# The last row block of an attention kernel, ended in two halves

## The chip, the cores and the metric

The kernel runs on one core of a Trainium2 chip. The metric is the device time of one launch in microseconds (us); lower is better. Five instruction streams take part and meet only at semaphores: TensorE (PE), VectorE (DVE), ScalarE (ACT), GpSimd (POOL), and SyncE (SP), which here issues only DMAs.

## The reference

Two layers of graph attention over N = 4096 nodes with D = 64 features, each followed by a residual sum and a layer norm without scale or shift:

```python
src, dst = h @ a1, h @ a2
e = leaky_relu(src[:, None] + dst[None, :], 0.01)
e = where(adj > 0, e, -9e15)               # layer 2: -1e9
h_prime = softmax(e, axis=1) @ h           # layer 2: @ (x @ weight_w), then + bias
x = layernorm(x + h_prime)                 # each row of 64 by itself
```

`adj` is 4096 x 4096 int32, about one entry in a thousand being 1. Layer 2 has the same form with `wh = x @ weight_w` in place of `h`. The output is x after layer 2, 4096 x 64 float32.

## The kernel before

The leaky relu makes exp(e) a product of a row factor and a column factor, with one pair of factors where src + dst is positive and another where it is not. So the masked softmax is two products of a 0/1 matrix with a small table: `pos` holds the mask where the sum is positive, `neg` where it is negative. Both are byte matrices that TensorE reads as fp8. The table `xy` (in layer 2 it lies in the buffer named `stage`) holds features and a column of ones, times the column factor, split into three bf16 parts: 3 x 65 = 195 columns.

**Tiling.** The rows come in `NS` = 8 blocks `s` of 512 rows; each has `RB` = 4 row blocks `r` of 128 rows, and each row block has a PSUM bank of its own, `acc[:, r]`. The 4096 columns come in `NG` = 4 granules `g` of 1024, each of 8 tiles of 128 columns. The function `granule(layer, s, g)` is TensorE's work on one granule: for each of the 4 row blocks 8 tiles x 2 masks = 16 matmuls of 195 columns, each with a weight load, into that row block's bank. In this text a **unit** is the 16 matmuls of one granule and one row block; a block `s` is 16 units, in the order g = 0 with r = 0 to 3, then g = 1, and so on. A bank is complete when all four granules have been added.

**Who makes what in layer 2.** For each block and granule:

- ACT (`signs`) writes 8 activations of sign into `neg[:, g]`, and raises `signs_ready`.
- DVE (`mask`) turns them into the two masks: an AND at L832 gives `neg`, an XOR at L835 gives `pos`; each has 128 x 1024 words.
- PE (`granule`) waits for both masks of that granule, before its first matmul.

After the last granule of a block the DVE does the epilogue: `read_acc` (L841, one reduction of a bank each, when that bank's last unit is done), `average` (L859 to L868), `residual_sum` (L873), `moments` (L878 to L881, ending in `var`); POOL computes var to the power -1/2 (L994, `inverse_std`); the DVE normalizes into `x1s` (L891, `normalize1`); SP stores `x1s` with one DMA of 128 KB (L293 in the loop, L295 for the last block). Instructions of `average` and later work on all 4 row blocks at once where they can (L859, L863), and one at a time where they can't (x4 at L866, L873, L878, L880, L891).

**Order.** Every engine runs its stream in the order written; nothing is scheduled. The blocks 1 to 7 of layer 2 are a loop on PE (L503); the DVE has a loop over s = 1 to 6 (L968), in which the masks of block s + 1 are woven with the epilogue of block s:

```python
with dve.Fori(1, NS - 1) as s:
    mask(1, s, NG - 1)
    for g in range(NG):
        if g:
            mask(1, s + 1, g - 1)
        if g == 1:
            read_acc(1, s)
        if g == 2:
            average(1, s); residual_sum(1, s); moments(1, s)
    normalize1(s)
```

So while PE works on block 7, the DVE does in this order: the rest of `read_acc` of block 6, the masks of granule 1 of block 7, the epilogue of block 6 up to `var`, the masks of granule 2, `normalize1` of block 6, the masks of granule 3. The masks of granule 0 come ahead of all that.

Of the kernel before, what the change touches and what calls it, by code (L numbers as in the profile page):

```python
# [23 lines left out]
ALU = mybir.AluOpType  # L24
# [10 lines left out]
P = 128  # L35
# [3 lines left out]
EPS = 1e-5  # L39
# [3 lines left out]
def gat_kernel(nc, x, adj, a0, w1, a1, bias1, ident, out):  # L43
# [28 lines left out]
    CODES = 0x38383838  # L72
    FREE_AT_FIRST = RING * RB
    LINKS = 8

    ctx = ExitStack()
    with ctx:
# [167 lines left out]
        @block.sync  # L245
        def _(sp):
            sp.sem_inc(stored, 16)
            load_tiles(sp, LOWER)
            sp.dma_start(acol[:, 0:1], a0[0:D, :]).then_inc(s_a, 16)
            load_rows(sp, slice(0, RB))  # L250
            load(sp, LOWER, 0, 0)
            load_rows(sp, slice(RB, IB // 2))
            load(sp, LOWER, 0, 1)
            sp.dma_start(acol[:, 1:2], a1[0:D, :]).then_inc(s_w, 16)
            sp.dma_start(acol[:, 2:3], a1[D:2 * D, :]).then_inc(s_w, 16)
            sp.dma_start(wext1[0:D, 0:D], w1).then_inc(s_w, 16)
# [24 lines left out]

            for g in range(KEEP, NG):
                sp.wait_ge(spilled[g - KEEP], 16 * NS)
                sp.wait_ge(pos_ready, (NS - 1) * NG + g + 1)
                reload(0, g)
            with sp.Fori(1, NS) as s:
                for g in range(KEEP, NG):
                    sp.wait_ge(pos_ready, (NS + s - 1) * NG + g + 1)
                    sp.sem_inc(sp_turn, 1)
                    reload(s, g)  # L290
                sp.wait_ge(x1_ready, NS + s + 1)
                sp.sem_inc(sp_turn, 1)
                sp.dma_start(rows_of(out, s - 1, RB, P), x1s[:, :, :]).then_inc(stored, 16)  # L293
            sp.wait_ge(x1_ready, 2 * NS + 1)
            sp.dma_start(rows_of(out, NS - 1, RB, P), x1s[:, :, :]).then_inc(stored, 16)  # L295
            sp.wait_ge(stored, 16 * (NS + 1))


        @block.tensor
        def _(pe):  # L300
# [114 lines left out]
                                            start=True, stop=True)  # L415
                last.then_inc(wh_ready, 1)

            def granule(layer, s, g):
                k = (layer * NS + s) * NG + g
                pe.wait_ge(neg_ready, k + 1)  # L420
                pe.wait_ge(pos_ready, k + 1)
                pe.sem_inc(pe_turn, 1)
                pe.wait_ge(tables_ready, layer * NG + g + 1)
                masks = [m[:, g, :].bitcast(FP8).rearrange("p (b i e) -> p b e i", b=GB, e=BYTES) for m in (pos, neg)]
                for r in range(RB):
                    if g == 0:
# [73 lines left out]
            scores1(NS - 2, NS)  # L500
            for g in range(1, NG):
                granule(1, 0, g)
            with pe.Fori(1, NS) as s:  # L503
                for g in range(NG):
                    granule(1, s, g)


        @block.scalar
# [153 lines left out]
        def _(dve):  # L662
# [171 lines left out]
                    dve.wait_ge(neg_ready, k + 1)  # L834
                    nc.vector.tensor_tensor(words(pos[:, g, :]), a, c, ALU.bitwise_xor).then_inc(pos_ready, 1)  # L835

            def read_acc(layer, s):
                for r in range(RB):

                    dve.wait_ge(products, FREE_AT_FIRST + ((layer * NS + s) * NG + NG - 1) * RB + r + 1)  # L840
                    nc.vector.tensor_reduce(  # L841
                        red[:, r, :, :].rearrange("p c f -> p (c f)").rearrange("p (c f) -> p c f", c=2),
                        acc[:, r, 0:2 * XW].rearrange("p (c k f) -> p c f k", c=2, k=PARTS), AX, ALU.add)\
                      .then_inc(acc_read, 1)

            def link(layer, s, n, ins):

                ins.then_inc(epi, 1)
                dve.wait_ge(epi, (layer * NS + s) * LINKS + n)

            V = nc.vector
            blocks = range(RB)

            def average(layer, s):

                factors = ab[:, :, :].rearrange("p c (k r h) -> p k h r c", r=RB, h=2)[:, bass.ds(s // 2, 1), bass.ds(s % 2, 1)]
                dve.wait_ge(acc_read, (layer * NS + s) * RB + 2 * RB)
                dve.wait_ge(exp_ready, [3, 6][layer])
                link(layer, s, 1, V.tensor_tensor(  # L859
                    red[:, :, :, :], red[:, :, :, :],  # L860
                    factors.rearrange("p k h r c -> p (k h r) c").unsqueeze(3).broadcast_to((P, RB, 2, E)), ALU.mult))
                dve.wait_ge(x1_ready, layer * NS + s + 1)
                link(layer, s, 2, V.tensor_tensor(num[:, :, :], red[:, :, 0, :], red[:, :, 1, :], ALU.add))  # L863
                link(layer, s, 3, V.tensor_scalar(empty, num[:, :, D], 0.0, None, ALU.is_equal))
                V.tensor_tensor(total, num[:, :, D], empty, ALU.add)
                link(layer, s, 4, [V.scalar_tensor_tensor(y[:, r, :], meanv[:, layer, :], empty[:, r:r + 1], y[:, r, :],  # L866
                                                          ALU.mult, ALU.add) for r in blocks][-1])
                V.reciprocal(rden, total).then_inc(epi, 1)  # L868

            def residual_sum(layer, s):  # L870

                dve.wait_ge(epi, (layer * NS + s) * LINKS + 5)
                link(layer, s, 6, [V.scalar_tensor_tensor(y[:, r, :], y[:, r, :], rden[:, r:r + 1],  # L873
                                                          xn[:, row_at(s, r), :].rearrange("p o d -> p (o d)"),
                                                          ALU.mult, ALU.add) for r in blocks][-1])

            def moments(layer, s):
                link(layer, s, 7, [V.bn_stats(bn[:, r, :], y[:, r, :]) for r in blocks][-1])  # L878
                dve.sem_inc(dve_turn, 1)
                link(layer, s, 8, [V.bn_aggr(mv[:, r, :], bn[:, r, :]) for r in blocks][-1])  # L880
                V.tensor_scalar(var, mv[:, :, 1], EPS, None, ALU.add).then_inc(var_ready, 1)  # L881
                if layer == 0:
                    V.tensor_scalar(minus_mean, mv[:, :, 0], -1.0, None, ALU.mult).then_inc(mean_turned, 1)

            def normalize1(s):

                dve.wait_ge(stored, 16 * (s + 1))
                dve.wait_ge(std_ready, 2 * NS + s + 1)
                dve.sem_inc(dve_turn, 1)
                for r in blocks:  # L890
                    last = V.tensor_scalar(x1s[:, r, :], y[:, r, :], mv[:, r, 0:1], rstd[:, r:r + 1],  # L891
                                           ALU.subtract, ALU.mult)
                last.then_inc(x1_ready, 1)
# [84 lines left out]
                        moments(1, s)  # L978
                normalize1(s)
            mask(1, NS - 1, NG - 1)  # L980
            read_acc(1, NS - 1)
            average(1, NS - 1)
            residual_sum(1, NS - 1)
            moments(1, NS - 1)
            normalize1(NS - 1)


        @block.gpsimd
        def _(pool):
            def inverse_std(layer, s):  # L990

                pool.wait_ge(var_ready, layer * NS + s + 1)
                pool.sem_inc(pool_turn, 1)
                nc.gpsimd.tensor_tensor(rstd, var, minus_half[:, :], ALU.pow).then_inc(std_ready, 1)  # L994
                if layer == 1:
                    return
                pool.wait_ge(std_ready, 2 * s + 1)
# [18 lines left out]
                inverse_std(0, s)  # L1016
                positive(s + 1, 3)
            inverse_std(0, NS - 1)
            with pool.Fori(0, NS) as s:
                inverse_std(1, s)  # L1020


# [20 lines left out]
```

## Time and profile before

| what | value |
|---|---|
| times of 3 runs | 504.74, 500.26, 503.65 us; median 503.65 |
| the profiled execution | 500.48 us; its span from first to last instruction 498.5 us |
| busy in the span | PE 443.1, PEld 414.0, DVE 409.3, ACT 394.9, POOL 86.8 us |
| matmuls of layer 2 (`acc<-stage`) | 2048, mean 248 ns each as recorded |
| mean granted TensorE clock | 0.932 of full |

All rows are of the one profiled execution. The time that a launch takes is its span and about 2 us around it. Recorded matmuls overlap one another: their length is not their cost, the distance from one start to the next is. In the DVE's rows a mark in brackets at the end is idle time before the row, and what ended it. "PEclk" is the TensorE clock that was granted: 1.00 is 2.4 GHz and 0.50 is 1.2 GHz.

### The profile page before, as it was taken

How to read it: one execution, taken by the hardware profiler on the slowest of the kernel's cores; microseconds unless marked ns; L12 is line 12 of the kernel's file. 1: busy time of each engine (PE TensorE's matmuls, PEld its weight loads, DVE VectorE, ACT ScalarE, POOL GpSimd, SP SyncE). 2: the span in 40 equal slices, each digit the busy share in tenths (PEclk: the TensorE clock that was granted, in tenths of full speed). 3: DMA queues.
4: the chain of work that ended last, by engine and by line, in shares of the span. 5: the costliest groups of instructions: out<-in, count | busy, mean ns of one | idle time of the engine just before them, and what ended most of it. 6: DMA issues, size and time to landing. Idle time of an engine off the chain costs nothing.

```text
span 498.5 us, 11757 instructions
## 1 busy us (share of the span) xinstructions
PE 443.1 (89%) x4420; PEld 414.0 (83%) x4420; DVE 409.3 (82%) x736; ACT 394.9 (79%) x589; POOL 86.8 (17%) x60
## 2 busy tenths in 40 slices
PE   0799868888989999998997959999999999999991
PEld 0379767877979889897997846999999999999991
DVE  3789989889799898998989897968587786968755
ACT  2686179878878879888794956999999999999920
POOL 0012221513315142241512120001010110101010
PEclk9987979997979979899899966999999999999997
DMA  7999999999999999999992200203030302022000
GB/s 193 246 240 279 278 263 286 321 297 303 324 309 322 305 299 318 319 331 302 331 310 93 81 0 2 60 27 96 1 95 0 95 0 95 17 77 84 10 11 11
DMA packets 80290, 87.64 MB, mean 176 GB/s; under 512 B 7298, under 2 KB 76162, under 8 KB 80258
## 3 DMA queue, kind: packets, MB, share of 16 engines
q1 hardware_dynamic: 45602, 52.98, 37.5%
q10 hardware_dynamic: 34656, 34.21, 25.2%
q8 instruction: 23, 0.38, 0.3%
q14 instruction: 9, 0.07, 0.0%
HBM read 77.74 MB, written 9.44 MB: 175 GB/s over the span
## 4 chain that ended last, share of the span: by engine, by line
PE 42%; DVE 24%; DMA 18%; issue 12%; POOL 1%; SPq 1%; ACT 1%; DVEq 0%; ACTq 0%; POOLq 0%
PE acc L431 38%; DMA stage<-in_adj 17%; DVE narrow L803 4%; DVE turned L815 4%; DVE pos L829 2%; DMA xn<-in_x 2%; DVE num L873 2%; DVE num L866 1%; DVE red L859 1%; PE flip L361 1%; DVE bn L878 1%; DVE num L863 1%; DVE kept L740 1%; PE acc L330 1%; DVE kept L737 1%
## 5 line engine op out<-in xcount | busy, mean ns | idle before, releaser
L569 ACT ACTIVATE neg<-srow,dcol 128x512 int8<-128x512 f32 (+1 forms) x320 | 221.4, 866 | 11.1 <-issue 7.6
L431 PE MATMUL acc<-xy_old,pos 128*128 128x195 bf16 x1024 | 196.0, 261 | 18.3 <-POOL pos L1007 12.2
L431 PE MATMUL acc<-xy_old,neg 128*128 128x195 bf16 x1024 | 195.7, 261 | 0.0
L431 PE MATMUL acc<-stage,pos 128*128 128x195 bf16 x1024 | 177.3, 248 | 0.0
L431 PE MATMUL acc<-stage,neg 128*128 128x195 bf16 x1024 | 177.3, 248 | 0.0
L569 ACT ACTIVATE neg<-xy_old,dcol 128x512 int8 x192 | 137.4, 863 | 0.0
L431 PEld LDWEIGHTS acc<-xy_old,pos 128*128 128x128 fp8e4 x1024 | 106.5, 104 | 26.8 <-issue 25.2
L431 PEld LDWEIGHTS acc<-xy_old,neg 128*128 128x128 fp8e4 x1024 | 106.0, 104 | 1.3
L431 PEld LDWEIGHTS acc<-stage,pos 128*128 128x128 fp8e4 x1024 | 100.6, 98 | 0.0
L431 PEld LDWEIGHTS acc<-stage,neg 128*128 128x128 fp8e4 x1024 | 100.4, 98 | 0.1
L803 DVE TENSOR_SCALAR narrow<-stage 128x4096 uint8<-128x4096 int32 x32 | 74.1, 2314 | 16.7 <-DMA stage<-in_adj 15.9
L994 POOL TENSOR_TENSOR small<-small,minus_half 128x4 f32<-128x4 f32 x16 | 35.1, 2192 | 209.0 <-DVE small L881 209.0
L841 DVE TENSOR_REDUCE red<-acc 128x130 f32<-128x390 f32 x64 | 33.7, 554 | 34.6 <-PE acc L431 34.5
L1007 POOL TENSOR_TENSOR pos<-kept,neg 128x512 uint32<-128x512 uint32 x16 | 22.2, 1390 | 142.7 <-DVE neg L832 142.7
L832 DVE TENSOR_TENSOR neg<-neg,kept 128x1024 uint32<-128x1024 uint32 x32 | 39.1, 1223 | 7.3 <-ACT neg L569 6.6
L832 DVE TENSOR_TENSOR neg<-neg,turned 128x1024 uint32<-128x1024 uint32 x32 | 39.1, 1223 | 2.4 <-ACT neg L569 1.7
L1007 POOL TENSOR_TENSOR pos<-turned,neg 128x512 uint32<-128x512 uint32 x16 | 22.3, 1393 | 54.6 <-DVE neg L832 53.8
L577 ACT ACTIVATE xn<-num,small 128x64 f32 (+1 forms) x32 | 11.5, 430 | 16.6 <-POOL small L1000 16.6
L319 PE MATMUL acc<-idf,xn 128*64 128x128 f32 x32 | 7.2, 421 | 15.2 <-DMA xn<-in_x 15.2
L319 PEld LDWEIGHTS acc<-idf,xn 128*64 128x64 f32 x32 | 5.3, 173 | 17.7 <-issue 11.9
L835 DVE TENSOR_TENSOR pos<-kept,neg 128x1024 uint32<-128x1024 uint32 x16 | 19.6, 1225 | 0.5
L835 DVE TENSOR_TENSOR pos<-turned,neg 128x1024 uint32<-128x1024 uint32 x16 | 19.6, 1224 | 0.5
(121 smaller groups left out, 343.0 us busy)
## 6 DMA issues: line engine op xcount, KB each, us to landing
stage<-in_adj ACTq DMA_DIRECT2D x64, 512.0 KB, 9.2
stage<-in_adj SPq DMA_DIRECT2D x64, 512.0 KB, 9.4
spill<-turned SPq DMA_DIRECT2D x16, 512.0 KB, 7.6
turned<-spill SPq DMA_DIRECT2D x16, 512.0 KB, 3.9
out<-x1s SPq DMA_DIRECT2D x8, 128.0 KB, 1.9
xn<-in_x SPq DMA_DIRECT2D x1, 768.0 KB, 16.5
kept<-in_x SPq DMA_DIRECT2D x4, 128.0 KB, 3.8
kept<-in_x ACTq DMA_DIRECT2D x4, 128.0 KB, 5.0
```

The lines of the kernel that those rows point to most:

```text
L319: last = nc.tensor.transpose(acc[0:D, t % RB, b * P:(b + 1) * P], xn[:, t // 2 * (2 * RB) + t % 2 + 2 * b, :], idf[:, :])
L431: last = nc.tensor.matmul(acc[:, r, c * XW:(c + 1) * XW], masks[c][:, t // BYTES, t % BYTES, r * P:(r + 1) * P], xy[layer][:, g * GT + t, ...
L569: last = nc.scalar.activation(o[:, t // BYTES, t % BYTES, :], row, ACT.Sign, bias=dcol[:, layer, col:col + 1])
L577: last = nc.scalar.activation(xn[:, row_at(s, r), :].rearrange("p o d -> p (o d)"), y[:, r, :], ACT.Identity, bias=shift_n[:, r:r + 1], sc ...
L803: nc.vector.tensor_scalar(narrow[:, 0:GN].rearrange("p (b g j) -> p g b j", b=GB, g=GR), stage[:, g % SLOTS, :].rearrange("p (g b j) -> p ...
L815: nc.vector.transpose(words(mask_at(s, g)), words(narrow[:, 0:GN])).then_inc(turned_ready, 1)
L829: nc.vector.scalar_tensor_tensor(words(pos[:, g, :])[:, half], c[:, half], CODES, a[:, half], ALU.bitwise_xor, ALU.bitwise_and).then_inc(p ...
L832: nc.vector.tensor_tensor(c, c, a, ALU.bitwise_and).then_inc(neg_ready, 1)
L835: nc.vector.tensor_tensor(words(pos[:, g, :]), a, c, ALU.bitwise_xor).then_inc(pos_ready, 1)
L841: nc.vector.tensor_reduce(red[:, r, :, :].rearrange("p c f -> p (c f)").rearrange("p (c f) -> p c f", c=2), acc[:, r, 0:2 * XW].rearrange( ...
L994: nc.gpsimd.tensor_tensor(rstd, var, minus_half[:, :], ALU.pow).then_inc(std_ready, 1)
L1007: nc.gpsimd.tensor_tensor(pos[:, g, :].bitcast(U32)[:, half], mask_at(s, g).bitcast(U32)[:, half], neg[:, g, :].bitcast(U32)[:, half], ALU ...
```

## The change

The last block of layer 2 (s = 7) is taken out of PE's loop and written out, its 16 units in another order: eight pieces of two units, each a granule for the row blocks 0 and 1 (h = 0) or 2 and 3 (h = 1). The epilogue of this block, POOL's power and the store run twice, each for two row blocks. Functions get a parameter `part` or `rows`; for all other blocks they issue what they did before. The semaphore counts are raised by one step for the second part.

```diff
+    HALVES = (slice(0, RB // 2), slice(RB // 2, RB))
+    LAST_ORDER = ((0, 0), (1, 0), (2, 0), (0, 1), (3, 0), (1, 1), (2, 1), (3, 1))
...
-            sp.wait_ge(x1_ready, 2 * NS + 1)
-            sp.dma_start(rows_of(out, NS - 1, RB, P), x1s[:, :, :]).then_inc(stored, 16)
-            sp.wait_ge(stored, 16 * (NS + 1))
+            for h, part in enumerate(HALVES):
+                sp.wait_ge(x1_ready, 2 * NS + 1 + h)
+                sp.dma_start(rows_of(out, NS - 1, RB, P)[:, part], x1s[:, part, :]).then_inc(stored, 16)
+            sp.wait_ge(stored, 16 * (NS + 2))
...
-            def granule(layer, s, g):
+            def granule(layer, s, g, rows=range(RB)):
...
-                for r in range(RB):
+                for r in rows:
...
-            with pe.Fori(1, NS) as s:
+            with pe.Fori(1, NS - 1) as s:
                 for g in range(NG):
                     granule(1, s, g)
+            for g, h in LAST_ORDER:
+                granule(1, NS - 1, g, range(RB)[HALVES[h]])
...
-            def read_acc(layer, s):
-                for r in range(RB):
-
-                    dve.wait_ge(products, FREE_AT_FIRST + ((layer * NS + s) * NG + NG - 1) * RB + r + 1)
+            def read_acc(layer, s, part=every):
+                for r in range(RB)[part]:
+
+                    dve.wait_ge(products, finished(layer, s, r))
...
             mask(1, NS - 1, NG - 1)
-            read_acc(1, NS - 1)
-            average(1, NS - 1)
-            residual_sum(1, NS - 1)
-            moments(1, NS - 1)
-            normalize1(NS - 1)
+            for part in HALVES:
+                read_acc(1, NS - 1, part)
+                average(1, NS - 1, part)
+                residual_sum(1, NS - 1, part)
+                moments(1, NS - 1, part)
+                normalize1(NS - 1, part)
...
-            with pool.Fori(0, NS) as s:
+            with pool.Fori(0, NS - 1) as s:
                 inverse_std(1, s)
+            for part in HALVES:
+                inverse_std(1, NS - 1, part)
```

(`finished` counts in `LAST_ORDER` which unit completes a bank.)

TensorE before, the body of the loop over blocks: the first matmul of each unit that waits, with its number in the stream (`stage` is the table of layer 2). Granules 1, 2 and 3 begin at 2470, 2534 and 2598, 64 matmuls apart.

```order
2403 L431 MATMUL acc<-stage,pos 128x195 [waits neg_ready,pos_ready,tables_ready,acc_read]
...
2420 L431 MATMUL acc<-stage,pos 128x195 [waits acc_read]
...
2470 L431 MATMUL acc<-stage,pos 128x195 [waits neg_ready,pos_ready,tables_ready]
...
2534 L431 MATMUL acc<-stage,pos 128x195 [waits neg_ready,pos_ready,tables_ready]
...
2598 L431 MATMUL acc<-stage,pos 128x195 [waits neg_ready,pos_ready,tables_ready]
```

TensorE now, the last block behind the loop, in the same form; each row that waits for the masks begins a piece of `LAST_ORDER`.

```order
2664 L434 MATMUL acc<-stage,pos 128x195 [waits neg_ready,pos_ready,tables_ready,acc_read]
...
2696 L434 MATMUL acc<-stage,pos 128x195 [waits neg_ready,pos_ready,tables_ready]
...
2728 L434 MATMUL acc<-stage,pos 128x195 [waits neg_ready,pos_ready,tables_ready]
...
2760 L434 MATMUL acc<-stage,pos 128x195 [waits neg_ready,pos_ready,tables_ready,acc_read]
...
2792 L434 MATMUL acc<-stage,pos 128x195 [waits neg_ready,pos_ready,tables_ready]
...
2824 L434 MATMUL acc<-stage,pos 128x195 [waits neg_ready,pos_ready,tables_ready]
```

The first need of granule 1's masks has moved from 64 matmuls after the block's start to 32, that of granule 2's from 128 to 64, and that of granule 3's (2792) from 192 to 128. What makes the masks has not moved.

The DVE before, at the end of its stream: the masks of granule 3 of the last block, then its epilogue for all four row blocks.

```order
L832 TENSOR_TENSOR neg<-neg,turned 128x1024
L835 TENSOR_TENSOR pos<-turned,neg 128x1024
L841 TENSOR_REDUCE red<-acc 128x130 x4
L859 TENSOR_TENSOR red<-red,ab 128x520
L863 TENSOR_TENSOR num<-red 128x260
L864 TENSOR_SCALAR small<-num 128x4
L865 TENSOR_TENSOR small<-num,small 128x4
L866 SCALAR_TENSOR_TENSOR num<-meanv,small,num 128x64 x4
```

The DVE now, the same place: the first part, from the masks to the sum, and the end of it with the start of the second part.

```order
L837 TENSOR_TENSOR neg<-neg,turned 128x1024
L840 TENSOR_TENSOR pos<-turned,neg 128x1024
L859 TENSOR_REDUCE red<-acc 128x130 x2
L878 TENSOR_TENSOR red<-red,ab 128x260
L880 TENSOR_TENSOR num<-red 128x130
...
L883 SCALAR_TENSOR_TENSOR num<-meanv,small,num 128x64 x2
...
L898 TENSOR_SCALAR small<-mv 128x2
L908 TENSOR_SCALAR x1s<-num,mv,small 128x64 x2
L859 TENSOR_REDUCE red<-acc 128x130 x2
```

The first part's rows stand wholly ahead of the second part's; behind the last matmul stands only the second, with half the elements or half the instructions at each step.

## Rows read from the trace of the kernel before

**Rows 1.** The chain that ended last, by time: start us, us, what.
```profile
454.95 33.47 PE acc L431 x387
```

**Rows 2.** Timeline of DVE while PE works on block 7: start us, us, what.
```profile
466.31 0.57 DVE L841 TENSOR_REDUCE red<-acc 128x130 f32<-128x390 f32 x1 [0.82 <-PE acc L431]
...
468.04 1.22 DVE L835 TENSOR_TENSOR pos<-kept,neg 128x1024 uint32<-128x1024 uint32 x1
469.18 0.69 DVE L859 TENSOR_TENSOR red<-red,ab 128x520 f32<-128x520 f32 x1
...
474.17 1.22 DVE L832 TENSOR_TENSOR neg<-neg,turned 128x1024 uint32<-128x1024 uint32 x1
475.43 1.23 DVE L835 TENSOR_TENSOR pos<-turned,neg 128x1024 uint32<-128x1024 uint32 x1
...
478.71 1.22 DVE L835 TENSOR_TENSOR pos<-turned,neg 128x1024 uint32<-128x1024 uint32 x1
```

**Rows 3.** Timeline of ACT from 460 us on: its last 24 signs.
```profile
459.22 17.31 ACT L569 ACTIVATE neg<-xy_old,dcol 128x512 int8 x24
```

**Rows 4.** Timeline of PE and of POOL around waits in layer 1.
```profile
66.37 0.32 PE L431 MATMUL acc<-xy_old,pos 128*128 128x195 bf16 x1 [6.29 <-POOL pos L1007]
66.49 0.37 PE L431 MATMUL acc<-xy_old,neg 128*128 128x195 bf16 x1
...
68.45 0.37 PE L431 MATMUL acc<-xy_old,neg 128*128 128x195 bf16 x1
...
82.12 1.27 POOL L1007 TENSOR_TENSOR pos<-kept,neg 128x512 uint32<-128x512 uint32 x1 [10.31 <-DVE neg L832]
83.50 0.24 PE L431 MATMUL acc<-xy_old,pos 128*128 128x195 bf16 x1 [1.80 <-POOL pos L1007]
```

**Rows 5.** Windows of PE: stretch, its us, PE busy (matmuls), PEclk, DMA share, GB/s.
```profile
60.08:65.30 5.22, 0.00 (x0) 1.00 0.91 295
...
66.37:72.00 5.63, 5.63 (x35) 0.50 1.11 268
...
112.67:114.88 2.21, 0.00 (x1) 0.59 1.12 304
114.88:119.90 5.02, 5.02 (x32) 0.50 1.07 338
...
236.00:239.35 3.35, 3.35 (x23) 0.50 1.12 360
263.32:265.23 1.91, 0.00 (x1) 1.00 0.00 0
```

**Rows 6.** Timeline of DVE, POOL and the DMA queue at the end.
```profile
484.30 0.56 DVE L841 TENSOR_REDUCE red<-acc 128x130 f32<-128x390 f32 x1 [4.37 <-PE acc L431]
...
488.45 0.56 DVE L841 TENSOR_REDUCE red<-acc 128x130 f32<-128x390 f32 x1 [0.82 <-PE acc L431]
489.05 0.70 DVE L859 TENSOR_TENSOR red<-red,ab 128x520 f32<-128x520 f32 x1
489.78 0.43 DVE L863 TENSOR_TENSOR num<-red 128x260 f32<-128x260 f32 x1
...
490.53 0.86 DVE L866 SCALAR_TENSOR_TENSOR num<-meanv,small,num 128x64 f32<-128x64 f32 x4
...
491.64 0.87 DVE L873 SCALAR_TENSOR_TENSOR num<-num,small,xn 128x64 f32<-128x64 f32 x4
492.55 0.61 DVE L878 BATCH_NORM_STATS2 bn<-num 128x6 f32<-128x64 f32 x4
493.31 0.38 DVE L880 BATCH_NORM_AGGREGATE mv<-bn 128x2 f32<-128x6 f32 x4 [0.15 <-DVE bn L878]
...
494.07 1.01 POOL L994 TENSOR_TENSOR small<-small,minus_half 128x4 f32<-128x4 f32 x1 [17.81 <-DVE small L881]
495.21 0.98 DVE L891 TENSOR_SCALAR x1s<-num,mv,small 128x64 f32<-128x64 f32 x4 [1.32 <-POOL small L994]
496.22 0.40 SPq L295 DMA_DIRECT2D out<-x1s  x1
```

More of the change, by code:

```diff
@@ L835, in mask, with finished @@
                     nc.vector.tensor_tensor(words(pos[:, g, :]), a, c, ALU.bitwise_xor).then_inc(pos_ready, 1)
-            def read_acc(layer, s):
-                for r in range(RB):
-                    dve.wait_ge(products, FREE_AT_FIRST + ((layer * NS + s) * NG + NG - 1) * RB + r + 1)
+            every = slice(0, RB)
+            def finished(layer, s, r):
+                if layer == 1 and isinstance(s, int) and s == NS - 1:
+                    done = 0
+                    for g, h in LAST_ORDER:
+                        for q in range(RB)[HALVES[h]]:
+                            done += 1
+                            if (g, q) == (NG - 1, r):
+                                return FREE_AT_FIRST + (layer * NS + s) * NG * RB + done
+                return FREE_AT_FIRST + ((layer * NS + s) * NG + NG - 1) * RB + r + 1
+            def read_acc(layer, s, part=every):
+                for r in range(RB)[part]:
+                    dve.wait_ge(products, finished(layer, s, r))
                     nc.vector.tensor_reduce(
@@ L844, in read_acc, with link, average @@
                       .then_inc(acc_read, 1)
-            def link(layer, s, n, ins):
+            def link(layer, s, n, ins, part=every):
                 ins.then_inc(epi, 1)
-                dve.wait_ge(epi, (layer * NS + s) * LINKS + n)
+                dve.wait_ge(epi, (layer * NS + s) * LINKS + n + (LINKS if part == HALVES[1] else 0))
             V = nc.vector
-            blocks = range(RB)
-            def average(layer, s):
+            def average(layer, s, part=every):
+                n = part.stop - part.start
@@ L856, in average @@
                 factors = ab[:, :, :].rearrange("p c (k r h) -> p k h r c", r=RB, h=2)[:, bass.ds(s // 2, 1), bass.ds(s % 2, 1)]
-                dve.wait_ge(acc_read, (layer * NS + s) * RB + 2 * RB)
+                factors = factors.rearrange("p k h r c -> p (k h r) c")[:, part].unsqueeze(3).broadcast_to((P, n, 2, E))
+                dve.wait_ge(acc_read, (layer * NS + s) * RB + RB + part.stop)
                 dve.wait_ge(exp_ready, [3, 6][layer])
-                link(layer, s, 1, V.tensor_tensor(
-                    red[:, :, :, :], red[:, :, :, :],
-                    factors.rearrange("p k h r c -> p (k h r) c").unsqueeze(3).broadcast_to((P, RB, 2, E)), ALU.mult))
+                link(layer, s, 1, V.tensor_tensor(red[:, part, :, :], red[:, part, :, :], factors, ALU.mult), part)
@@ L862, in average @@
                 dve.wait_ge(x1_ready, layer * NS + s + 1)
-                link(layer, s, 2, V.tensor_tensor(num[:, :, :], red[:, :, 0, :], red[:, :, 1, :], ALU.add))
-                link(layer, s, 3, V.tensor_scalar(empty, num[:, :, D], 0.0, None, ALU.is_equal))
-                V.tensor_tensor(total, num[:, :, D], empty, ALU.add)
+                link(layer, s, 2, V.tensor_tensor(num[:, part, :], red[:, part, 0, :], red[:, part, 1, :], ALU.add), part)
+                link(layer, s, 3, V.tensor_scalar(empty[:, part], num[:, part, D], 0.0, None, ALU.is_equal), part)
@@ L866, in average @@
+                V.tensor_tensor(total[:, part], num[:, part, D], empty[:, part], ALU.add)
                 link(layer, s, 4, [V.scalar_tensor_tensor(y[:, r, :], meanv[:, layer, :], empty[:, r:r + 1], y[:, r, :],
[L867 to L872, printed above, removed]
+                                                          ALU.mult, ALU.add) for r in range(RB)[part]][-1], part)
@@ L873, in residual_sum @@
+                V.reciprocal(rden[:, part], total[:, part]).then_inc(epi, 1)
+            def residual_sum(layer, s, part=every):
+                dve.wait_ge(epi, (layer * NS + s) * LINKS + 5 + (LINKS if part == HALVES[1] else 0))
                 link(layer, s, 6, [V.scalar_tensor_tensor(y[:, r, :], y[:, r, :], rden[:, r:r + 1],
                                                           xn[:, row_at(s, r), :].rearrange("p o d -> p (o d)"),
-                                                          ALU.mult, ALU.add) for r in blocks][-1])
@@ L877, in moments @@
-            def moments(layer, s):
-                link(layer, s, 7, [V.bn_stats(bn[:, r, :], y[:, r, :]) for r in blocks][-1])
+                                                          ALU.mult, ALU.add) for r in range(RB)[part]][-1], part)
+            def moments(layer, s, part=every):
+                link(layer, s, 7, [V.bn_stats(bn[:, r, :], y[:, r, :]) for r in range(RB)[part]][-1], part)
                 dve.sem_inc(dve_turn, 1)
-                link(layer, s, 8, [V.bn_aggr(mv[:, r, :], bn[:, r, :]) for r in blocks][-1])
-                V.tensor_scalar(var, mv[:, :, 1], EPS, None, ALU.add).then_inc(var_ready, 1)
+                link(layer, s, 8, [V.bn_aggr(mv[:, r, :], bn[:, r, :]) for r in range(RB)[part]][-1], part)
+                V.tensor_scalar(var[:, part], mv[:, part, 1], EPS, None, ALU.add).then_inc(var_ready, 1)
@@ L882, in moments, with normalize1 @@
                 if layer == 0:
                     V.tensor_scalar(minus_mean, mv[:, :, 0], -1.0, None, ALU.mult).then_inc(mean_turned, 1)
-            def normalize1(s):
+            def normalize1(s, part=every):
                 dve.wait_ge(stored, 16 * (s + 1))
-                dve.wait_ge(std_ready, 2 * NS + s + 1)
+                dve.wait_ge(std_ready, 2 * NS + s + 1 + (1 if part == HALVES[1] else 0))
                 dve.sem_inc(dve_turn, 1)
-                for r in blocks:
+                for r in range(RB)[part]:
@@ L980, in _, with inverse_std @@
             mask(1, NS - 1, NG - 1)
-            read_acc(1, NS - 1)
-            average(1, NS - 1)
-            residual_sum(1, NS - 1)
-            moments(1, NS - 1)
-            normalize1(NS - 1)
+            for part in HALVES:
[4 more added lines that the diff above has]
+                normalize1(NS - 1, part)
         @block.gpsimd
         def _(pool):
-            def inverse_std(layer, s):
-                pool.wait_ge(var_ready, layer * NS + s + 1)
+            def inverse_std(layer, s, part=slice(0, RB)):
+                pool.wait_ge(var_ready, layer * NS + s + 1 + (1 if part == HALVES[1] else 0))
                 pool.sem_inc(pool_turn, 1)
-                nc.gpsimd.tensor_tensor(rstd, var, minus_half[:, :], ALU.pow).then_inc(std_ready, 1)
+                nc.gpsimd.tensor_tensor(rstd[:, part], var[:, part], minus_half[:, part], ALU.pow).then_inc(std_ready, 1)
                 if layer == 1:
```

## The prediction

> **What bounds the kernel now.** I read the end of the chain that ended last first, since the change touches only the last block. From 454.95 us on, 33.47 us of the chain are matmuls of L431 without a break [rows 1]; behind them come the last reduction and the epilogue [rows 6]. So two stretches set the end: the sixteen units of block 7 on PE, and the tail behind the last of them.
>
> The pace of PE comes from the four reductions of block 7. Each starts as soon as its bank is complete, the first at 484.30 and the fourth at 488.45 us [rows 6]: 4.15 / 3 = 1.383 us a unit, 86.4 ns a matmul, sixteen units 22.1 us. The fourth reduction of block 6 starts at 466.31 us [rows 2], and 466.31 + 22.13 = 488.44: PE goes through block 7 without waiting. Then comes the tail: from 488.45 to the store's issue at 496.22 us are 7.77 us [rows 6], and 2.28 us more to the end of the span at 498.5.
>
> The second thing to read is when the masks of block 7 become ready. In its timeline the DVE ends the XOR of granule 1 at 468.04 + 1.22 = 469.26 us. From 469.18 to 474.17 us it does the epilogue of block 6, back to back. The XOR of granule 2 ends at 475.43 + 1.23 = 476.66, that of granule 3 at 478.71 + 1.22 = 479.93 [rows 2]. That is in time for the order of before: a unit's first matmul starts about 0.2 us ahead of the end of the matmuls before it (L431's records overlap), so block 7 starts at about 466.1, granule 1 at 471.6, granule 2 at 477.2 and granule 3 at 482.7. Granule 2's masks have 0.5 us to spare. No row shows this as a wait, and so the busy shares hide it.
>
> **The change, part by part.** All sums are made on the profiled execution.
>
> *The order of the units.* What PE needs when, in the new order: granule 1 after two units, granule 2 after four, granule 3 after eight. It starts at 466.1 us.
>
> - Granule 1 would start at 466.1 + 2.77 = 468.87. Its masks are ready at 469.26. How fast PE follows shows in layer 1: POOL ended a mask at 82.12 + 1.27 = 83.39 and the matmul started at 83.50 [rows 4], 0.11 us later. So it starts at 469.37, a wait of 0.5 us.
> - Its 32 matmuls end their issue at 469.37 + 2.77 = 472.14. Granule 2's masks are ready at 476.66, so the next starts at 476.77: a wait of 4.63 us.
> - Granule 0 for the second half needs nothing new. Granule 3 would start at 476.77 + 5.53 = 482.3, and its masks are there at 479.93: no wait.
>
> The waits sum to 5.1 us. Everything behind is twelve units without a wait, and PE's end goes from 488.4 to 493.5 us. This is on the path. The wait can't be filled, because each engine keeps its order: the DVE does the epilogue of block 6 ahead of granule 2's masks as before, and the change gives it nothing else to do. Nor is ACT the cause: its last 24 activations end at 459.22 + 17.31 = 476.53 us [rows 3], so the eight of granule 2 end two thirds in, at about 470.8, over 3 us before the DVE takes them.
>
> *The loop.* Block 7's matmuls are now new code behind a loop. The trace shows no such place on PE. If it costs anything it does so at the start of block 7, and then it lies inside the wait for granule 2's masks, which hides up to 4.6 us of it. I put it at nothing, and up to 1 us if that wait were not there.
>
> *The tail behind the last unit.* The first part's epilogue begins when granule 3 has gone through row blocks 0 and 1, six units and 8.3 us before PE's end. It takes what the second takes, some 5.5 us (worked out next), so it is over before the second part's last bank is complete. Its own cost is covered, with about 1.4 us to spare to row block 2's reduction. The second part's cost, from rows 6: the five groups of four instructions (0.86, 0.87, 0.61, 0.38 and 0.98 us, together 3.70) have two each, and save 1.85. L859 goes from 128x520 (0.70 us) to the size of L863 (0.43), and saves 0.27. L863 goes to 128x130, for which there is no row; by the slope between the two, 0.27 us for 260 elements, it saves 0.13. The small instructions on 128x4 and POOL's power (1.01) have half the elements, but sizes this small cost what any instruction costs; I take no gain. The store has 64 KB in place of 128: of its 2.28 us I take 0.1 off. Together 2.35 us. Bounds: 1.85 if the wide ones gain nothing, 3.2 if POOL halves and the store saves 0.4.
>
> So much for the order and the tail: 5.13 - 2.35 = 2.8 us slower.
>
> *The clock.* TensorE's granted clock falls after idle stretches in this trace. After the wait of 6.29 us in layer 1 the matmuls start at 0.50, that is 1.2 GHz, and stay there for 5.63 us; a wait of 2.21 us, ahead of which lie eight small matmuls and another wait of that size, led to 5.02 us of it; there are two more stretches behind places with little work, one of 3.35 us and one about as long as the first (not shown) [rows 4, 5]. Against a fall: in the long wait the clock stood at 1.00 for 5.22 us before it went, and a full wait of 1.91 us left it at 1.00 [rows 5]. A wait of 4.63 us, with the 0.5 us one 2.8 us ahead of it, lies between. I take it that the clock falls, since two waits half as long, close together, were enough, and since the longest time at full clock in an idle stretch ended without PE having to work. Its cost: at half clock the twelve matmuls from 66.49 to 68.45 us are 163 ns apart [rows 4] against 86.4, so each us at half clock loses 1 - 86.4 / 163 = 0.47 us. The three stretches in the rows have a mean of 4.67 us: 2.2 us; from the shortest to the longest 1.6 to 2.65. The twelve units left are long enough to take all of it.
>
> The Trainium skill has a rule that speaks against this change: in TensorE: Matmul & The Clock Gate, section "HAM oscillation — how this bites in real kernels", groups of matmuls with a few us of waiting between them fall back to the lower clock in each wait and begin the next group slow. By that rule the sum is the one with the clock's term; the rows at 112.67 and 66.37 us agree, the row at 263.32 shows a wait too short for it.
>
> Forecast: 5.13 + 2.2 - 2.35 = 5.0 us slower. The profiled execution would go from 500.48 to 505.5; from the median of the runs, 3.2 us above it, 503.65 goes to **508.6 us**.
>
> **Rivals.**
>
> *The clock stays up.* The 5.22 us at 1.00 in an idle stretch speak for it. Then 2.8 us: 506.4.
>
> *The masks come in time and the tail is all that is left.* This is the case that ends faster: 503.65 - 2.35 = 501.3. It needs granule 2's masks by 472.1, 4.5 us earlier than the DVE makes them. Even if the DVE took them as soon as ACT had finished, at 470.8, two instructions of 1.22 us put them at 473.3, and PE would wait 1.2 us; the net would then be 0.7 us faster. The time decides at a total wait of 2.35 us: below it the change gains. Only an execution in which the DVE is well ahead of PE would do so, and here the DVE's order behind block 6's last reduction is tied to PE: that reduction at 466.31, then 10.35 us of DVE work without idle to 476.66 [rows 2]. I see no way to it but a misreading.
>
> *The parts get in each other's way.* If the first epilogue is not over by the second part's first reduction, the second starts late by the excess: with a first part as long as the whole of before, 7.77 us from 485.2, it ends at 493.0 and delays the last reductions by about 0.6 us. Or more of the clock than rows show. Some 6 to 6.5 us: up to 510.2.
>
> **How the numbers follow.** Clock falls 0.68; clock stays 0.22; in time, faster 0.04; more than that 0.06. A measurement of this kernel can tell about 1% (5.0 us) from no change: its three runs lie 4.5 us apart. The forecast lies just at that edge, so the case with the clock is split about evenly by its own bounds (5.13 + 1.6 - 3.2 = 3.5 to 5.13 + 2.65 - 1.85 = 5.9 us): slower by over 1% 0.34 + 0.06 + a little = 0.42, within 1% 0.34 + 0.22 - a little = 0.55, faster by over 1% 0.03. The likeliest case's range is 507.1 to 509.6; with the case without the clock (506.4, down to 505.5 with the larger gain in the tail) and the third above, 505.3 to 510.3.
>
> **What would show it.** In the timeline of PE in block 7: a wait of about 4.6 us on the DVE's `pos` two units after one of 0.5 us, with the DVE's masks at the same distance from block 6's last reduction as before (10.35 us); the granted clock at 0.50 for 3 to 6 us behind it; PE's end 27 to 30 us after that reduction instead of 22.1. In the DVE's: two epilogues, the first ended before row block 2's reduction, the second some 5.5 us from its last reduction's start to the store's issue. The prediction is wrong if PE goes through block 7 without a break, or if the second epilogue is no shorter than the whole one.

## The result, and the profile after

The changed kernel takes 507.5 us (median of 4 runs, 505.67 to 509.44), the kernel before 502.54 us (4 runs, 500.26 to 504.74). The ratio is 1.0124 with a 95% interval of 1.0084 to 1.0165: about 1.2% slower. The profiled execution has a span of 506.3 us against 498.5.

That difference of 7.8 us isn't all from the change. The two executions are already 2.45 us apart when block 6's last reduction starts: at 466.31 us before [rows 2], at 468.76 after. Up to there every engine's work and its order are the same in both, and over the eleven executions profiled here this point lies anywhere between 464.1 and 471.0 us, in no order that fits the edits. So everything below is measured from it. From the start of block 6's last reduction to the end of the span it is 498.5 - 466.31 = 32.19 us before and 506.3 - 468.76 = 37.54 us after: 5.35 us more. I call this stretch **the last stretch**. The profile gives spans to 0.1 us, so a difference between two last stretches is good to about 0.1 us.

The timeline of the DVE after (start us, us, what); L859 is the reduction of a bank, L837 and L840 are the AND and the XOR of a mask, L908 is the normalization:

```profile
468.76 0.56 DVE L859 TENSOR_REDUCE red<-acc 128x130 f32<-128x390 f32 x1 [0.82 <-PE acc L434]
...
470.49 1.23 DVE L840 TENSOR_TENSOR pos<-kept,neg 128x1024 uint32<-128x1024 uint32 x1
471.63 0.69 DVE L878 TENSOR_TENSOR red<-red,ab 128x520 f32<-128x520 f32 x1
...
477.88 1.23 DVE L840 TENSOR_TENSOR pos<-turned,neg 128x1024 uint32<-128x1024 uint32 x1
...
489.11 0.56 DVE L859 TENSOR_REDUCE red<-acc 128x130 f32<-128x390 f32 x1 [6.72 <-PE acc L434]
490.49 0.56 DVE L859 TENSOR_REDUCE red<-acc 128x130 f32<-128x390 f32 x1 [0.82 <-PE acc L434]
491.09 0.43 DVE L878 TENSOR_TENSOR red<-red,ab 128x260 f32<-128x260 f32 x1
491.55 0.29 DVE L880 TENSOR_TENSOR num<-red 128x130 f32<-128x130 f32 x1
...
495.35 0.54 DVE L908 TENSOR_SCALAR x1s<-num,mv,small 128x64 f32<-128x64 f32 x2 [1.01 <-POOL small L1012]
497.40 0.56 DVE L859 TENSOR_REDUCE red<-acc 128x130 f32<-128x390 f32 x1 [1.51 <-PE acc L434]
498.79 0.56 DVE L859 TENSOR_REDUCE red<-acc 128x130 f32<-128x390 f32 x1 [0.82 <-PE acc L434]
```

The masks of granule 2 end at 477.88 + 1.23 = 479.11, that is 10.35 us behind 468.76, exactly as before [rows 2]. The DVE has not moved; PE's need has. PE's timeline has two gaps in block 7:

```profile
471.82 0.24 PE L434 MATMUL acc<-stage,pos 128*128 128x195 bf16 x1 [0.33 <-issue]
...
479.21 0.32 PE L434 MATMUL acc<-stage,pos 128*128 128x195 bf16 x1 [4.46 <-DVE pos L840]
```

The first is the wait for granule 1's masks: the profile puts it down to "issue", but the matmul starts 0.10 us behind the end of their XOR at 470.49 + 1.23 = 471.72. The second is the wait for granule 2's. Behind the second the windows of PE (stretch, its us, busy, PEclk, DMA share, GB/s) show the clock:

```profile
477.00:478.00 1.00, 0.00 (x0) 1.00 0.00 0
478.00:479.00 1.00, 0.00 (x0) 0.66 0.00 0
479.00:480.00 1.00, 0.79 (x6) 0.50 0.00 0
...
484.00:485.00 1.00, 1.00 (x8) 0.50 0.00 0
485.00:486.00 1.00, 1.00 (x13) 0.92 0.00 0
486.00:487.00 1.00, 1.00 (x14) 1.00 0.00 0
```

It falls from 2.4 to 1.2 GHz inside the wait and comes back at about 485.1, so the first 5.9 us behind the wait run at half clock. In the chain of the changed kernel the last twelve units (192 matmuls) take 19.56 us:

```profile
479.21 19.56 PE acc L434 x192
```

The tail from the last reduction's start at 498.79 to the second store's issue, and POOL's two powers (these replace rows 6):

```profile
494.52 0.69 POOL L1012 TENSOR_TENSOR small<-small,minus_half 128x2 f32<-128x2 f32 x1 [15.81 <-DVE small L898]
502.80 0.70 POOL L1012 TENSOR_TENSOR small<-small,minus_half 128x2 f32<-128x2 f32 x1 [7.59 <-DVE small L898]
...
504.20 0.38 SPq L298 DMA_DIRECT2D out<-x1s  x1
```

From the last reduction to the store's issue it is 5.41 us in place of 7.77, and the store takes 506.3 - 504.20 = 2.10 us in place of 2.28.

### The profile page after: what moved, and what is told of

It reads as the page before. It is cut to its first block, busy times and chain, and to the rows that moved or that the text cites. A ratio compares the mean times of both kernels' runs of the same rounds, so it can differ in the third digit from the quotient of the medians.

```text
span 506.3 us, 11765 instructions
## 1 busy us (share of the span) xinstructions
PE 451.2 (89%) x4420; PEld 419.4 (83%) x4420; DVE 411.2 (81%) x742; ACT 395.1 (78%) x589; POOL 87.2 (17%) x61
## 4 chain that ended last, share of the span: by engine, by line
PE 43%; DVE 24%; DMA 18%; issue 12%; POOL 1%; SPq 1%; ACT 1%; DVEq 0%; POOLq 0%; ACTq 0%
PE acc L434 39%; DMA stage<-in_adj 16%; DVE narrow L808 4%; DVE turned L820 3%; DVE pos L834 2%; DMA xn<-in_x 2%; DVE num L883 2%; DVE num L890 1%; DVE red L878 1%; PE flip L364 1%; DVE neg L837 1%; DVE bn L895 1%; DVE num L880 1%; DVE kept L745 1%; PE acc L333 1%
## 5 line engine op out<-in xcount | busy, mean ns | idle before, releaser
L434 PE MATMUL acc<-xy_old,pos 128*128 128x195 bf16 x1024 | 198.5, 263 | 17.4 <-POOL pos L1025 12.2
L434 PE MATMUL acc<-xy_old,neg 128*128 128x195 bf16 x1024 | 198.1, 263 | 0.0
L434 PE MATMUL acc<-stage,pos 128*128 128x195 bf16 x1024 | 180.5, 250 | 4.8 <-DVE pos L840 4.5
L434 PE MATMUL acc<-stage,neg 128*128 128x195 bf16 x1024 | 180.4, 251 | 0.0
L1012 POOL TENSOR_TENSOR small<-small,minus_half 128x4 f32<-128x4 f32 (+1 forms) x17 | 35.5, 2086 | 217.9 <-DVE small L898 217.9
L859 DVE TENSOR_REDUCE red<-acc 128x130 f32<-128x390 f32 x64 | 33.7, 554 | 38.2 <-PE acc L434 38.2
L837 DVE TENSOR_TENSOR neg<-neg,kept 128x1024 uint32<-128x1024 uint32 x32 | 39.1, 1222 | 7.6 <-ACT neg L574 7.0
L837 DVE TENSOR_TENSOR neg<-neg,turned 128x1024 uint32<-128x1024 uint32 x32 | 39.1, 1223 | 2.4 <-ACT neg L574 1.7
L840 DVE TENSOR_TENSOR pos<-turned,neg 128x1024 uint32<-128x1024 uint32 x16 | 19.6, 1225 | 0.5
L840 DVE TENSOR_TENSOR pos<-kept,neg 128x1024 uint32<-128x1024 uint32 x16 | 19.6, 1225 | 0.5
```

What stands on the lines that cost most here:

```text
L434: last = nc.tensor.matmul(acc[:, r, c * XW:(c + 1) * XW], masks[c][:, t // BYTES, t % BYTES, r * P:(r + 1) * P], xy[layer][:, g * GT + t, ...
L837: nc.vector.tensor_tensor(c, c, a, ALU.bitwise_and).then_inc(neg_ready, 1)
L859: nc.vector.tensor_reduce(red[:, r, :, :].rearrange("p c f -> p (c f)").rearrange("p (c f) -> p c f", c=2), acc[:, r, 0:2 * XW].rearrange( ...
L1012: nc.gpsimd.tensor_tensor(rstd[:, part], var[:, part], minus_half[:, part], ALU.pow).then_inc(std_ready, 1)
```

## The experiments

In each row both kernels ran on the same chip. "Last stretch" is read from one profiled execution of that kernel.

| kernel | median us (runs) | before there (runs) | ratio, 95% interval | last stretch us | against 32.19 |
|---|---|---|---|---|---|
| the change | 507.5 (4) | 502.54 (4) | 1.0124, 1.0084 to 1.0165 | 37.54 | +5.35 |
| e1 unrolled only | 503.13 (10) | 501.38 (25) | 1.0017, 0.9985 to 1.0049 | 32.28 | +0.09 |
| e2 order only | 509.15 (4) | 501.38 (25) | 1.0151, 1.0111 to 1.0191 | 39.88 | +7.69 |
| e3 two ends only | 502.85 (11) | 501.38 (25) | 1.0021, 0.9995 to 1.0047 | 32.61 | +0.42 |
| e4 wait filled | 503.98 (10) | 501.38 (25) | 1.0048, 1.002 to 1.0076 | 34.75 | +2.56 |
| e5 masks in time | 499.09 (11) | 502.15 (20) | 0.994, 0.9919 to 0.9962 | 30.00 | -2.19 |
| e6 masks first | 507.48 (6) | 502.15 (20) | 1.009, 1.0057 to 1.0122 | 36.81 | +4.62 |
| e7 in time, woven | 498.83 (8) | 502.15 (20) | 0.9927, 0.9901 to 0.9953 | 29.69 | -2.50 |
| e8 masks first, again | 503.18 (10) | 501.95 (19) | 1.0018, 0.9979 to 1.0057 | 33.07 | +0.88 |
| e9 wait half filled | 505.02 (10) | 501.95 (19) | 1.0058, 1.0034 to 1.0083 | 34.69 | +2.50 |

Divided by 502 us, the last column falls inside the interval of the ratio beside it in every row, so the differences in the totals agree with those of the last stretch within the noise. For e5 and e7 the median shows a larger gain (0.6 and 0.7%) than the last stretch (0.4 and 0.5%).

**e1, the unrolling alone.** Order, epilogue and store are those of before.

```diff
-    LAST_ORDER = ((0, 0), (1, 0), (2, 0), (0, 1), (3, 0), (1, 1), (2, 1), (3, 1))
+    LAST_ORDER = ((0, 0), (0, 1), (1, 0), (1, 1), (2, 0), (2, 1), (3, 0), (3, 1))
-            for part in HALVES:
+            for part in (every,):
```

(and the same for the store and POOL.)

> Only the unrolling: block 7 stands behind PE's loop as in the changed kernel, its units are in the order of before, and there is one epilogue and one store. If the late masks are the cause, nothing changes: 32.2 us from the start of block 6's last reduction to the end of the span, as before (466.31 to 498.5), and the total within 0.5% of before. Rival: new code behind a loop costs PE something; then a gap shows on PE at the start of block 7 and the stretch is 33 us or more.

32.28 us, the ratio does not differ from 1, and there is no gap on PE in block 7. New code behind a loop costs nothing here.

**e2, the order alone.** The changed `LAST_ORDER`, with one epilogue and one store.

> Only the order of the units, with one epilogue and one store: the waits and the clock's loss without the shorter tail. Theory (waits 5.1 us, clock 2.2 to 3.0 us, the tail worth 2.5 us by itself): from block 6's last reduction to the end of the span 32.2 + 7.9 = 40.1 us, some 1.6% slower than before. Rival: the epilogue in two parts gains nothing or costs something; then this kernel is as fast as the changed one, 37.5 us in that stretch.

39.88 us. Its profile has the same two gaps, and the clock at half behind the second:

```profile
475.97 0.32 PE L434 MATMUL acc<-stage,pos 128*128 128x195 bf16 x1 [4.46 <-DVE pos L840]
```

The order costs 7.7 us here, and the difference to the change is 39.88 - 37.54 = 2.3 us. The halved tail is worth a little more than that: from the last reduction's start to the end of the span are 505.4 - 495.27 = 10.1 us here and 506.3 - 498.79 = 7.5 in the change. PE ended 0.3 us earlier here, because behind the same wait the clock was at half for 5.4 us (to about 481.3) in place of 5.9.

**e3, the two ends alone.** The changed kernel with the order of units of e1.

> Only the epilogue and store in two parts, with the units in the order of before. PE's end is where it was. The first part can start only 14 units into the block and takes 5.4 us from its last reduction, so it ends 24.8 us behind block 6's last reduction, when PE is long done (22.1); then come two reductions (0.6 us to the start of the second) and 5.4 us and the store of 2.1: 32.9 us in the stretch, 0.7 us more than before, within 0.5% in the total. Rival: halving pays by itself; then the stretch is 29.7 us, 0.5% faster.

32.61 us, 0.4 more than before and 0.3 less than expected. The DVE's timeline shows what a split without a reordering runs into:

```profile
483.47 0.56 DVE L859 TENSOR_REDUCE red<-acc 128x130 f32<-128x390 f32 x1 [0.82 <-PE acc L434]
...
488.34 0.54 DVE L908 TENSOR_SCALAR x1s<-num,mv,small 128x64 f32<-128x64 f32 x2 [1.01 <-POOL small L1012]
488.79 1.03 DVE L859 TENSOR_REDUCE red<-acc 128x130 f32<-128x390 f32 x2
```

The last two reductions stand back to back behind the first epilogue, with no wait for PE: PE finished some 2.6 us earlier (with the pace of before its last bank is complete 22.14 us behind 464.09, at 486.2; its last matmul starts at 485.95). So the split alone gains nothing.

**e4, the wait filled with matmuls.** 50 matmuls more, their result is never read.

```diff
             for g, h in LAST_ORDER:
+                if (g, h) == (2, 0):
+                    for n in range(50):
+                        nc.tensor.matmul(flip[:, 0:XW], onesN[:, :].bitcast(BF16)[:, 0:P],
+                                         xy[1][:, 0, 0].rearrange("p k f -> p (k f)"), start=True, stop=True)
                 granule(1, NS - 1, g, range(RB)[HALVES[h]])
```

> The changed kernel with 50 more matmuls (195 columns, into an unused bank, their result is not read) put where PE waits for granule 2's masks: 50 x 86.4 ns = 4.3 us, inside the wait of 4.46 us. They are work left without a result, and the wait ends when it did. If the clock's fall is a part of the loss, the granted clock stays at 1.00 and the stretch from block 6's last reduction to the end goes from 37.5 to 34.6 us (loss of the clock 19.56 - 192 x 0.0864 = 3.0 us). Rival: the twelve units behind the wait are slow for another reason than the clock (new code, the changed order of banks); then the stretch stays at 37.5 us.

34.75 us. The chain of e4 has the filler and then the same twelve units:

```profile
475.24 4.21 PE flip L512 x50
479.70 16.77 PE acc L434 x192
```

The last twelve units start at the same place, 479.70 - 469.25 = 10.45 us behind block 6's last reduction (after: 479.21 - 468.76 = 10.45), and take 16.77 instead of 19.56 us. The granted clock is 1.00 throughout. So the clock's share of the loss is 19.56 - 16.77 = 2.79 us in this pair of executions, and useless work on PE recovers it. The rival, a slowness of the new code or order, is out.

**e9, the wait half filled.** As e4 with `range(25)`.

> The changed kernel with 25 more matmuls (195 columns, result not read) in the wait for granule 2's masks: they fill 2.2 us of it, and about 2.2 us stay idle. The wait ends when it did. If an idle stretch of that length leaves the clock at 1.00, the stretch from block 6's last reduction to the end is 34.7 us, as with 50 matmuls; if it falls as in the changed kernel, 37.5 us. The rows of before had both: 1.91 us left it up, 2.21 us behind a thinly filled place did not. I lean to the first.

34.69 us: as with 50. The wait that is left, 2.35 us, does not bring the clock down; it stays at 1.00:

```profile
478.25 0.24 PE L434 MATMUL acc<-stage,pos 128*128 128x195 bf16 x1 [2.35 <-DVE pos L844]
```

**e5, the masks in time.** Granules 0 and 1 for all row blocks, then 2 and 3 by halves.

```diff
-    LAST_ORDER = ((0, 0), (1, 0), (2, 0), (0, 1), (3, 0), (1, 1), (2, 1), (3, 1))
+    LAST_ORDER = ((0, 0), (0, 1), (1, 0), (1, 1), (2, 0), (3, 0), (2, 1), (3, 1))
```

> The changed kernel with another order of the eight pieces: granules 0 and 1 for all row blocks first, then granules 2 and 3 for row blocks 0 and 1, then 2 and 3 for the others. Granule 2 is needed 8 units in, as in the kernel before (its masks are 0.5 us early there), granule 3 10 units in, 13.8 us, when its masks are ready to within 0.1 us. Theory: no wait of PE above 0.2 us, the clock stays at 1.00, the first part's epilogue ends about when PE does (16.7 + 5.4 = 22.1 us behind block 6's last reduction), and the second part ends at 22.1 + 0.6 + 5.4 + 2.1 = 30.2 us: 2.0 us less than before, 0.4% faster. Rival: any order but the old one costs PE its pace or its clock; then the stretch is 33 us or more.

30.00 us, and 0.6% faster than the kernel before (ratio 0.994, all of its interval below 1). PE has no gap in block 7. This is the idea of the change with the second half's pieces of granules 0 and 1 moved ahead of granule 2. What is left of a collision is in the DVE's timeline:

```profile
486.57 0.54 DVE L908 TENSOR_SCALAR x1s<-num,mv,small 128x64 f32<-128x64 f32 x2 [1.01 <-POOL small L1012]
487.02 1.03 DVE L859 TENSOR_REDUCE red<-acc 128x130 f32<-128x390 f32 x2
```

The first epilogue, which waits 1.01 us for POOL, ends at about the time when the last bank is complete (465.00 + 22.14 = 487.14), and both reductions of the second part stand behind it.

**e7, in time and woven.** The order of units is that of e5, and row block 2's reduction is put where the first part waits for POOL.

```diff
+                if h == 0:
+                    read_acc(1, NS - 1, slice(2, 3))
                 normalize1(NS - 1, part)
```

(and the second part reads only row block 3 first.)

> As the kernel with the masks in time, but the reduction of row block 2 stands between the first part's moments and its normalization, where the DVE otherwise waits for POOL, and the second part reads only row block 3 afterwards. Theory: the second part's last reduction starts as soon as its bank is complete, 22.3 us behind block 6's last reduction, and the end is at 22.3 + 5.4 + 2.1 = 29.8 us, 0.4 us less than without it; 0.5% faster than before. Rival: the reduction comes too late for the gap and delays the first part; then 30.2 us or more.

29.69 us, 0.3 less than e5 in the profile:

```profile
489.06 0.56 DVE L859 TENSOR_REDUCE red<-acc 128x130 f32<-128x390 f32 x1 [0.28 <-PE acc L434]
489.79 0.54 DVE L908 TENSOR_SCALAR x1s<-num,mv,small 128x64 f32<-128x64 f32 x2 [0.17 <-POOL small L1017]
490.44 0.56 DVE L859 TENSOR_REDUCE red<-acc 128x130 f32<-128x390 f32 x1
```

The reduction fits; POOL is then waited for 0.17 us instead of 1.01. The ratios of e5 and e7 overlap, so that step is shown by the timeline alone. It is the fastest kernel here: 0.7% faster than before.

**e6 and e8, the masks first.** These keep the changed order and move the DVE instead: in the iteration of block 6, now written out, `mask(1, 7, 2)` stands ahead of block 6's epilogue.

```diff
+            s = NS - 2
+            mask(1, s, NG - 1)
+            mask(1, s + 1, 0)
+            read_acc(1, s)
+            mask(1, s + 1, 1)
+            mask(1, s + 1, 2)
+            average(1, s)
+            residual_sum(1, s)
+            moments(1, s)
+            normalize1(s)
             mask(1, NS - 1, NG - 1)
```

> The changed kernel, and in the DVE's block 6 the masks of granule 2 of block 7 stand ahead of block 6's epilogue. PE's order stays as changed. If the DVE's order is what made the wait, granule 2's masks come 2.6 us behind ACT's signs, the wait of 4.46 us becomes about 1.2 us, and granule 3's masks, now later than block 6's epilogue, cost about 1.9 us: waits of 3.6 us together, the clock stays at 1.00, and the stretch from block 6's last reduction to the end is 32.2 + 3.6 - 2.5 = 33.3 us, 0.2% slower than before. If the clock falls all the same, 36 us. Rival: the wait comes from ACT's pace; then it stays above 4 us.

36.81 us, 3.5 more than I had expected. The wait for granule 2's masks did shrink from 4.46 to 1.11 us, so it is the DVE's order that makes it; but the wait for granule 3's is 3.76 us, and the clock fell in it (below, the windows of PE):

```profile
478.08 0.24 PE L434 MATMUL acc<-stage,pos 128*128 128x195 bf16 x1 [1.11 <-DVE pos L840]
...
487.54 0.32 PE L434 MATMUL acc<-stage,pos 128*128 128x195 bf16 x1 [3.76 <-DVE pos L840]
```

```profile
487.00:488.00 1.00, 0.46 (x4) 0.68 0.01 3
488.00:489.00 1.00, 1.00 (x9) 0.50 0.00 0
...
490.00:491.00 1.00, 1.00 (x9) 0.61 0.00 0
```

Granule 3's masks came later than I had worked out:

```profile
484.06 0.98 DVE L908 TENSOR_SCALAR x1s<-num,mv,small 128x64 f32<-128x64 f32 x4 [1.32 <-POOL small L1022]
484.96 1.22 DVE L837 TENSOR_TENSOR neg<-neg,turned 128x1024 uint32<-128x1024 uint32 x1
486.21 1.22 DVE L840 TENSOR_TENSOR pos<-turned,neg 128x1024 uint32<-128x1024 uint32 x1
```

I had left out the normalization ahead of them, 0.98 us and 1.32 us of waiting for POOL, which the mask of granule 2 used to cover. e8 puts the masks of granule 3 ahead of `normalize1(s)`:

> As the kernel with the masks first, but the masks of granule 3 now stand ahead of block 6's normalization, which waits for POOL. The masks of granule 2 stay at 7.0 us behind block 6's last reduction; block 6's moments end at 11.75 us there, so granule 3's masks are ready at 14.2 us. PE waits 0.3, 1.3 and about 1.6 us. If the clock needs a longer idle stretch to fall, it stays at 1.00: twelve units after 7.1 us and the wait put the second part's last reduction at 25.5 us and the end of the span at 33.0 us, 0.2% slower than before. If several short waits bring it down too, 34.6 us or more.

33.07 us. Its two waits on masks are

```profile
474.02 0.24 PE L434 MATMUL acc<-stage,pos 128*128 128x195 bf16 x1 [1.11 <-DVE pos L840]
...
481.26 0.24 PE L434 MATMUL acc<-stage,pos 128*128 128x195 bf16 x1 [1.55 <-DVE pos L840]
```

and the clock stays at 1.00 through both. Against e6 that is 3.7 us less: 2.2 of wait (3.76 - 1.55) and, by the rate of the prediction, 3.2 x 0.47 = 1.5 of clock. With the waits short, the changed order comes within 0.9 us of the kernel before, but it doesn't gain: ACT's signs allow granule 2's masks no earlier (ahead of them the DVE waits 1.55 us for ACT in e6 and in e8).

## Why the prediction was right

**The masks' place and the waits: right to a few hundredths.** The step said that granule 1 starts 3.06 us behind block 6's last reduction and granule 2 10.46 us behind it; measured are 471.82 - 468.76 = 3.06 and 479.21 - 468.76 = 10.45. (The profile calls these waits 0.33 and 4.46 us, where I had 0.5 and 4.63: it counts from the end of the last record, and that end lies 0.17 us behind the start that the next matmul would have had.) That the DVE's order is the cause is shown by e6 and e8, where moving one pair of instructions took the wait from 4.46 to 1.11 us, and by e5, where needing them later removed it.

**The clock: right in kind, too small in size.** It fell, as taken to be the likeliest. The term was 2.2 us, worked out from a mean of 4.67 us at half clock; here it was 5.9 us, and e4 prices it at 2.79 us. 5.9 x 0.47 gives 2.8, so the rate per us was right and the length was off; it lies just above the bound of 2.65 that I gave, and PE's end, 498.79 - 468.76 = 30.03 us behind block 6's last reduction, just above my 27 to 30. The length was not to be had from a mean: behind the same wait of 4.46 us it was 5.4 us in e2.

**The tail: nearly right, by two errors that cancel.** I had 2.25 us up to the store's issue and 0.1 for the store, 2.35 together; measured are 2.36 (7.77 - 5.41) and 0.18, 2.54 together. But the groups of four save less than half: x2 take 0.47, 0.48, 0.35, 0.25 and 0.54 us where I had halved 0.86, 0.87, 0.61, 0.38 and 0.98: two instructions take more than half of what four take. They save 1.61 us instead of 1.85. POOL's power, which I had taken as unchanged, went from 1.01 to 0.70 us and made up for it; that it would was not foreseen. The wide ones came out as worked out (0.43, and 0.29 for 128x130).

**The loop: nothing**, as said, and e1 shows it without the wait that would have hidden it.

**The sum.** The waits alone moved PE's end by 496.50 - 469.25 - 22.14 = 5.11 us in e4, where the clock stays up (its last reduction starts at 496.50, block 6's at 469.25); I had 5.13. 5.11 + 2.79 - 2.54 = 5.36, measured 5.35 in the last stretch, where I had 5.0: the clock's term was 0.6 us too small and the tail's 0.2. The forecast of 508.6 us was worked out from a median of 503.65; with the median of the runs now at hand, 502.54, the same sum gives 507.5, the time measured. That it agrees to a tenth is luck: the interval of the ratio is 2 us wide to each side. The chance of slower by over 1% was put at 0.42, and it came out at 1.2%; but the last stretch alone is 5.35 / 502.5 = 1.06%, so the edge was as near as it looked.

**The rivals.** With the clock up the change would have cost 2.6 us (e4), where 2.8 was said. The case with the masks in time was said to be worth -2.35 us; e5, which makes it true by another order, has -2.19, and e7 -2.50. The prediction saw no way to it: it asked only for earlier masks, not for an order that needs them later. And the 0.7 us that I thought could be gained with granule 2's masks taken as soon as ACT allows left out that granule 3's masks then come later: e8, the better of the two tries, loses 0.88. The parts don't get in each other's way in the change (the second part's first reduction waits 1.51 us for PE) but do in e3 and, a little, in e5. The 0.6 us that I gave this rival was misread: a first part that ends at 493.0 has both reductions behind it, and where they stand back to back (e3) the two take 1.03 us together, so the last would start at about 493.5, when its bank is complete, and lose next to nothing.

## What to carry to other kernels

An order that finishes some outputs early asks for every input earlier; work out, for each input, when its maker delivers it and when the new order first needs it. Here a maker (the DVE, with granule 2's masks) with 0.5 us to spare was asked for its product 5 us earlier, and no row of waits in the old profile showed it, since slack leaves no idle time. Once the pieces are placed by those two lists of times, the same idea gains: 0.6% with e5 (0.4 to 0.8% by its interval) instead of a loss of 1.2%.

A wait of TensorE can cost more than its length, because of the clock behind it: here 2.8 us on top of the 5.1 us of waits. The wait could be removed by another order (e5); left as it is, 25 matmuls without use inside it bought those 2.8 us back (e9).

## What the runs showed of the hardware

- TensorE's clock stayed at 1.00 through waits of 1.11, 1.55 and 2.35 us between dense matmuls (e8, e9), and fell in waits of 3.76 us (e6) and 4.46 us (the change, e2). After it fell, the matmuls ran at half clock for 3.2 us in e6, 5.4 us in e2 and 5.9 us in the change. In the kernel before the clock also fell in a wait of 2.21 us [rows 5], but ahead of that one lay only eight small matmuls and another wait of 2.41 us.
- POOL's power on 128x4 takes 1.01 us when the DVE is idle and 1.94 us in the loop, where the DVE works on masks at the same time; e6 and e8 show the two for the same block 6: 1.01 us with the DVE waiting, 1.91 us with granule 3's masks beside it. On 128x2 it takes 0.70. Why so small an instruction gets shorter by nearly a third with half the elements, while the DVE's stay at 0.17 us (128x4 and 128x2 alike), was not tried.
- The spread of the totals (497.8 to 505.9 us for kernels with the same last stretch as before) seems to arise before block 7: in the profiled executions the last stretch of e1 repeats that of before to 0.1 us, while over all kernels the point where it begins varies by up to 7 us. What makes it vary stays open.
